# A decoder block in float32 on one core: every stage of cross-attention behind the row scaling runs one slot sooner

## What is computed

```python
x = x + attn(layernorm(x))            # 16 heads of 64, over each batch's 128 tokens
x = x + xattn(layernorm(x), ctx)      # 16 heads of 16, keys and values from ctx, a mask over keys
x = x + ffn(layernorm(x))             # 8 experts, 256 -> 512 -> 256, all summed, gated by one norm_g
```

## Time and profile before

| | |
|---|---|
| median of 3 runs | 855.11 us (855.07 to 857.67) |
| the profiled execution: its time | 854.01 us |
| the profiled execution: its span | 852.2 us |
| busy share of the span | PE 96%, PEld 83%, ACT 56%, DVE 53%, POOL 27% |
| mean granted TensorE clock | 0.992 of full |
| first and last scores of cross-attention (L819) | 320.0 and 466.5 us |

### The profile page before, as it was taken

How to read it: one execution, slowest core, us unless ns; L and a number is a source line. 1 busy time by engine, 2 the same in 40 slices (tenths; PEclk the granted TensorE clock), 3 DMA queues, 4 the chain that set the end, 5 groups by cost and what they waited for, 6 DMA issues and landing times.

```text
span 852.2 us, 16891 instructions
## 1 busy us (share of the span) xinstructions
PE 817.1 (96%) x6171; PEld 711.1 (83%) x6171; DVE 447.7 (53%) x935; ACT 476.8 (56%) x1532; POOL 227.4 (27%) x221
## 2 busy tenths in 40 slices
PE   9999999999999987999887999999999999999998
PEld 7778888888888875777775899999999899999997
DVE  4564664564555548899988554552233322433223
ACT  5555555455464546777777467544544454444543
POOL 3443343123233444668575400000000000000000
PEclk9999999999999999999998999999999999999999
DMA  6311000000000065666471233100000000000000
GB/s 193 108 51 39 1 2 2 2 1 2 2 25 2 2 151 146 167 144 179 99 195 51 62 100 99 50 26 2 1 1 2 25 0 0 0 25 1 1 1 25
DMA packets 22889, 42.22 MB, mean 50 GB/s; under 512 B 3352, under 2 KB 3872, under 8 KB 22816
## 3 DMA queue, kind: packets, MB, share of 16 engines
q1 hardware_dynamic: 21936, 40.64, 17.6%
q10 hardware_dynamic: 880, 0.60, 0.3%
HBM read 30.35 MB, written 10.49 MB: 48 GB/s over the span
## 4 chain that ended last, share of the span: by engine, by line
PE 81%; DVE 9%; DMA 3%; issue 3%; ACT 2%; POOL 2%; SPq 0%; POOLq 0%; ACTq 0%; DVEq 0%
PE Y L720 27%; PE A L720 25%; PE S L720 11%; PE T L847 5%; PE S L838 3%; PE O L881 3%; ACT probs L1127 2%; DMA arena<-stage 2%; DVE probs L1300 1%; DVE nm L1291 1%; PE S L819 1%; DVE xn L1231 1%; DMA stage<-arena 1%; PE O L868 1%; PE S L949 1%
## 5 line engine op out<-in xcount | busy, mean ns | idle before, releaser
L1127 ACT ACTIVATE probs<-S,nm 128x128 f32<-128x128 f32 x512 | 180.5, 378 | 127.3 <-DVE nm L1291 127.2
L720 PEld LDWEIGHTS Y<-arena,PT 128*128 128x128 f32 x1536 | 199.9, 191 | 11.4 <-DVE PT L1203 1.4
L1203 DVE TENSOR_TENSOR PT<-probs,PT 128x512 fp32r<-128x512 f32 x128 | 89.7, 702 | 227.5 <-ACT PT L1183 227.5
L720 PE MATMUL Y<-arena,PT 128*128 128x256 f32 x1536 | 203.8, 283 | 0.4
L1551 POOL TENSOR_TENSOR probs<-probs,rinv 128x512 f32<-128x512 f32 x128 | 134.3, 1049 | 236.3 <-DVE rinv L1296 236.3
L720 PE MATMUL A<-XT,arena 128*128 128x512 f32 x612 | 159.2, 394 | 0.0
L1183 ACT ACTIVATE PT<-probs 128x512 fp32r<-128x512 f32 x128 | 80.8, 631 | 106.9 <-PE Y L720 106.5
L1300 DVE COPY probs<-T 128x512 f32<-128x512 f32 x96 | 66.0, 688 | 113.3 <-PE T L847 112.9
L720 PEld LDWEIGHTS A<-XT,arena 128*128 128x128 f32 x612 | 108.1, 189 | 17.9
L1127 ACT ACTIVATION_READ_ACCUMULATOR probs<-S,nm 128x1 f32 x512 | 111.2, 217 | 0.0
L720 PE MATMUL S<-XT,arena 128*128 128x512 f32 x384 | 99.7, 395 | 0.0
(11 more groups left out here) (124 smaller groups left out, 996.4 us busy)
## 6 DMA issues: line engine op xcount, KB each, us to landing
wst<-in_pieces SPq DMA_DIRECT2D x43, 256.0 KB, 2.6
stage<-arena SPq DMA_DIRECT2D x32, 256.0 KB, 2.8
arena<-stage SPq DMA_DIRECT2D x51, 128.0 KB, 3.9
arena<-stage SPq DMA_DIRECT2D x21, 256.0 KB, 3.9
craw<-in_ctxT SPq DMA_DIRECT2D x4, 512.0 KB, 4.1
out<-craw SPq DMA_DIRECT2D x8, 256.0 KB, 2.0
xs<-in_x SPq DMA_DIRECT2D x3, 512.0 KB, 5.4
craw<-in_pieces SPq DMA_DIRECT2D x6, 256.0 KB, 2.6
```

The lines of the kernel that those rows point to most:

```text
L720: mm = pe.matmul(acc, lhs[a], rhs[b], start=first and i == 0, stop=last and i == 2, skip_group_check=shared)
L1127: last = act.activation(probs[:, ring(ph, g, n), u * P:(u + 1) * P], S[n % 2][:, u * P:(u + 1) * P], ACT.Exp, bias=nm[:, n % 4, u:u + 1], ...
L1203: dve.tensor_tensor(out_, src, hi.bitcast(F32), ALU.subtract).then_inc(sem_, 1)
```

## The change

In the phase 1 stages behind the normalisation, every lag goes down by one: the transposes from 3 to 2, the copies from 4 to 3, PV, `out` and `out_hi` from 5 to 4, `out_low` from 6 to 5, projection, residual and bias from 6 to 5. The scores, maxima, exponentials, inverses and the normalisation keep theirs, and so does the place of each stage in its engine's order within a slot. No instruction is added or removed, and no semaphore is changed. The diff of the tables (where an entry stands for several like it, one is shown):

```diff
         PE_ORDER = (
...
-            (("pv", "cross", (0, 5)), ("scores", "cross", (0, 0)), ("proj", "proj", (3, 6)),
+            (("pv", "cross", (0, 4)), ("scores", "cross", (0, 0)), ("proj", "proj", (3, 5)),
              ("xt1", "xt1", (0, 0)), ("v", "v", (0, 0)), ("qk", "qk", (0, 0)),
-             ("xt0", "xt0", (0, 0)), ("transpose", "cross", (0, 3))),
+             ("xt0", "xt0", (0, 0)), ("transpose", "cross", (0, 2))),
...
         DVE_ORDER = (
...
-            (("probs", "cross", (0, 4)), ("inverse", "cross", (0, 2)), ("out", "cross", (0, 5)),
+            (("probs", "cross", (0, 3)), ("inverse", "cross", (0, 2)), ("out", "cross", (0, 4)),
              ("max", "cross", (0, 0)), ("xt1", "xt1_out", (0, 0)),
              ("qk", "q_out", (0, 0)), ("xt0", "xt0_out", (0, 0)), ("stats", "stats", (0, 0)),
-             ("aggr", "aggr", (0, 0)), ("norm", "norm", (0, 0)), ("residual", "residual", (3, 6))),
+             ("aggr", "aggr", (0, 0)), ("norm", "norm", (0, 0)), ("residual", "residual", (3, 5))),
...
         POOL_ORDER = (
-            (("normalise", "quad", (1, 2)), ("out_hi", "cross", (0, 5)), ("out_low", "cross", (0, 6)),
-             ("bias", "bias", (3, 6)), ("aggr", "aggr", (0, 0)),
+            (("normalise", "quad", (1, 2)), ("out_hi", "cross", (0, 4)), ("out_low", "cross", (0, 5)),
+             ("bias", "bias", (3, 5)), ("aggr", "aggr", (0, 0)),
              ("ctx", "ctx", (0, 0))),
```

More of the change, by code:

```diff
@@ L513, in build @@
              ("scores", "even", (0, 0)), ("pv", "odd", (1, 0)), ("transpose", "even", (1, 0)),
-             ("proj", "proj", (3, 6))),
-            (("pv", "cross", (0, 5)), ("scores", "cross", (0, 0)), ("proj", "proj", (3, 6)),
+             ("proj", "proj", (3, 5))),
+            (("pv", "cross", (0, 4)), ("scores", "cross", (0, 0)), ("proj", "proj", (3, 5)),
              ("xt1", "xt1", (0, 0)), ("v", "v", (0, 0)), ("qk", "qk", (0, 0)),
[1 row of a table removed]
[1 row of a table added]
             (("xt1", "xt1", (0, 0)), ("qk", "qk", (0, 0)), ("v", "v", (0, 0)), ("xt0", "xt0", (0, 0))),
-            (("scores", "cross", (0, 0)), ("proj", "proj", (3, 6)), ("pv", "cross", (0, 5)),
-             ("transpose", "cross", (0, 3)), ("v", "v", (0, 0)), ("qk", "qk", (0, 0))),
-            (("transpose", "odd", (1, 0)), ("proj", "proj", (3, 6)), ("v", "v", (0, 0)),
+            (("scores", "cross", (0, 0)), ("proj", "proj", (3, 5)), ("pv", "cross", (0, 4)),
+             ("transpose", "cross", (0, 2)), ("v", "v", (0, 0)), ("qk", "qk", (0, 0))),
+            (("transpose", "odd", (1, 0)), ("proj", "proj", (3, 5)), ("v", "v", (0, 0)),
              ("pv", "odd", (1, 0)), ("scores", "cross", (0, 0))),
@@ L538, in build @@
              ("qk", "q_out", (0, 0)), ("max", "even", (0, 0)), ("out", "odd", (1, 0)),
-             ("inverse", "even", (0, 0)), ("out_low", "odd", (1, 0)), ("residual", "residual", (3, 6)),
+             ("inverse", "even", (0, 0)), ("out_low", "odd", (1, 0)), ("residual", "residual", (3, 5)),
              ("stats", "stats", (0, 0)), ("aggr", "aggr", (0, 0)), ("norm", "norm", (0, 0))),
-            (("probs", "cross", (0, 4)), ("inverse", "cross", (0, 2)), ("out", "cross", (0, 5)),
+            (("probs", "cross", (0, 3)), ("inverse", "cross", (0, 2)), ("out", "cross", (0, 4)),
              ("max", "cross", (0, 0)), ("xt1", "xt1_out", (0, 0)),
              ("qk", "q_out", (0, 0)), ("xt0", "xt0_out", (0, 0)), ("stats", "stats", (0, 0)),
-             ("aggr", "aggr", (0, 0)), ("norm", "norm", (0, 0)), ("residual", "residual", (3, 6))),
+             ("aggr", "aggr", (0, 0)), ("norm", "norm", (0, 0)), ("residual", "residual", (3, 5))),
             (("xt1", "xt1_out", (0, 0)), ("qk", "q_out", (0, 0)),
@@ L547, in build @@
              ("xt0", "xt0_out", (0, 0))),
-            (("inverse", "cross", (0, 2)), ("out", "cross", (0, 5)), ("probs", "cross", (0, 4)),
+            (("inverse", "cross", (0, 2)), ("out", "cross", (0, 4)), ("probs", "cross", (0, 3)),
              ("max", "cross", (0, 0)), ("qk", "q_out", (0, 0)),
-             ("residual", "residual", (3, 6)), ("stats", "stats", (0, 0)), ("aggr", "aggr", (0, 0)),
+             ("residual", "residual", (3, 5)), ("stats", "stats", (0, 0)), ("aggr", "aggr", (0, 0)),
              ("norm", "norm", (0, 0))),
@@ L555, in build @@
         POOL_ORDER = (
-            (("normalise", "quad", (1, 2)), ("out_hi", "cross", (0, 5)), ("out_low", "cross", (0, 6)),
-             ("bias", "bias", (3, 6)), ("aggr", "aggr", (0, 0)),
+            (("normalise", "quad", (1, 2)), ("out_hi", "cross", (0, 4)), ("out_low", "cross", (0, 5)),
+             ("bias", "bias", (3, 5)), ("aggr", "aggr", (0, 0)),
              ("ctx", "ctx", (0, 0))),
-            (("normalise", "quad", (1, 2)), ("out_hi", "cross", (0, 5)), ("out_low", "cross", (0, 6)),
-             ("bias", "bias", (3, 6)), ("aggr", "aggr", (0, 0)),
+            (("normalise", "quad", (1, 2)), ("out_hi", "cross", (0, 4)), ("out_low", "cross", (0, 5)),
+             ("bias", "bias", (3, 5)), ("aggr", "aggr", (0, 0)),
              ("ctx", "ctx", (0, 0))),
             (("aggr", "aggr", (0, 0)),),
-            (("normalise", "quad", (1, 2)), ("out_hi", "cross", (0, 5)), ("out_low", "cross", (0, 6)),
-             ("bias", "bias", (3, 6)), ("aggr", "aggr", (0, 0)),
+            (("normalise", "quad", (1, 2)), ("out_hi", "cross", (0, 4)), ("out_low", "cross", (0, 5)),
+             ("bias", "bias", (3, 5)), ("aggr", "aggr", (0, 0)),
              ("ctx", "ctx", (0, 0))),
-            (("normalise", "quad", (1, 2)), ("blank", "blank", (0, 0)), ("out_hi", "cross", (0, 5)),
-             ("out_low", "cross", (0, 6)), ("ctx", "ctx", (0, 0))))
+            (("normalise", "quad", (1, 2)), ("blank", "blank", (0, 0)), ("out_hi", "cross", (0, 4)),
+             ("out_low", "cross", (0, 5)), ("ctx", "ctx", (0, 0))))
         block = ctx.enter_context(nc.Block())
```

## The result

The changed kernel takes 893.2 us (median of four runs, 891.6 to 894.9) against 856.3 beside it: 1.042 times the time of the kernel before, interval 1.038 to 1.046. Run again it gave 1.0419 (1.0391 to 1.0447). The forecast was 885.5 with a range of 869 to 901. The profiled execution took 891.6 with a span of 889.8, which is 37.6 over the span of before.

What follows compares the result with a forecast made beforehand. PE was taken as nearly the bound before, a one-slot ring of 2.64 us after the change. Terms of 16.9, 8.5, 0.5, 1.1 and 3.4 sum to 30.4; with 855.1 that gave 885.5 us, range 869 to 901.

Steps and rivals of the forecast that it cites:

- term 1: The 48 steady slots each hold the whole ring of 2.64 us: 126.7 us against 109.84, +16.9.
- a ring of one slot: Normalisation, transposes, copy and inverse wait for each other within one slot, 2.64 us; before, the ring closed over two slots.
- Term 2: Crowded slots 0, 6, 12 (14 in the second group) and 15 outlast the ring and no longer average out: +8.5.
- Term 3: The opening: quad 0's transposes stand before quad 3's scores, one set of 0.56 us in that path: +0.5.
- Term 4: The drain, to the last transposes: they come one slot sooner, but longer slots use that up: +1.1.
- Term 5: Behind the last transposes: only one expert block runs beside the output chain, PE waits before the projection: +3.4.
- The fall of the clock: Rival: PE's waits lower its clock for some three slots in each of four passes, +12, 897 us; chance 0.13.
- "Faster": Rival: the ring's links overlap, under 2.29 us, and the pipeline ends one slot sooner: 853 us; chance 0.02.
- "even": Rival: only light slots feel the ring and the terms cancel against a sooner end, within 2.6 us; chance 0.02.
- The normalisations: Sign: their starts stand 2.6 to 2.7 us apart in plain slots, 3.8 to 4 in slots 6 and 12.

Runs made afterwards that it cites:

- one swap: VectorE's inverse put ahead of the copy in the changed kernel: 867.8 us, 1.016; the same in the kernel before: 853.7 us, 0.997.
- a dose: GpSimd's normalisation in two halves, 1.18 us for 1.04: on the changed kernel 899.9 us, 1.0515; on the kernel before 852.2 us, 0.997.
- the repeat: The changed kernel run once more with nothing altered: 892.4 us, 1.0419.
- the filler: Changed kernel plus unused matmuls of ones before drain transposes: 890.7 us, 1.040; placed again (eight before quad 10, none before 11, 15): 891.1 us, 1.0405.

## Why the prediction was right, and where it was short

- **The mechanism and term 1** held: a ring of one slot, 2.64 us forecast, 2.64 to 2.65 measured, opened by one swap and, in plain slots, lengthened one for one by a dose.
- **Term 2** was forecast at 8.5; over 48 x 2.64 the stretch took 9.5. Most crowded slots came out as costed. In slot 6 the residual now follows the low half:

```profile
395.74 0.74 DVE L1275 SCALAR_TENSOR_TENSOR arena<-A,bias,arena 128x512 fp32r<-128x512 f32 x1
396.40 1.28 DVE L1331 TENSOR_TENSOR xs<-Y,xs 128x512 f32<-128x512 f32 x2
397.60 0.68 DVE L1300 COPY probs<-T 128x512 f32<-128x512 f32 x1
398.19 0.17 DVE L1296 RECIPROCAL rinv<-rsum 128x4 f32<-128x4 f32 x1
```

  From normalisation to normalisation there (394.67 to 398.44) are 3.77, +1.13 as forecast. Slot 12 gave +1.19 and +1.22 for +1.28, but +0.67 in the last group's pass, where no context is left to cast and only the power stands before the normalisation. Slot 15 gave +0.59 for +0.64, and slot 0 had the short pair of xn, GpSimd being idle (in slot 15, with `out_low` on GpSimd, it was 2.22):

```profile
379.04 1.09 DVE L1231 TENSOR_SCALAR xn<-xs,mv,rstd 128x256 f32<-128x256 f32 x2
```

  What I hadn't counted are two small ones, 0.19 in slot 2 (PE's projection and transposed tokens) and 0.17 in slot 14 (GpSimd's `out_hi` and context), and one slot in the fourth group's pass in which the clock fell: 3.91 for 2.64. Taking each pass where its clock held, apart from the opening's tail, 44.5 and 45.6 us here and 44.9 in the repeat, the 48 slots come to 134.9, against 135.2 forecast. That is closer than the parts deserve: the 0.6 too much for the last slot 12 and the 0.7 of small ones left out nearly cancel. In the five profiles of this stretch the clock fell one to three times, 0.9 to 1.3 us each.
- **Term 3** was short, 0.5 for 2.0. I priced a set of transposes only. They stand ahead of the next scores, and they waited for a normalisation that itself stood behind layernorm's power; PE's clock had fallen in that wait (it falls in the opening of the kernel before as well, 0.50 in 332:334):

```profile
330.69 1.11 PE L847 MATMUL T<-ident,probs 128*128 128x128 f32 x4 [2.13 <-POOL probs L1551]
331.74 1.08 PE L868 MATMUL O<-probs,wst 128*32 128x128 f32 x16
...
332.75 0.80 PE L819 MATMUL S<-dropped,identr 128*128 128x512 f32 x1
```

  How much of the 2.0 is the change stays open: in the five profiles of the changed opening the second group's first maximum comes at 331.9 to 334.4, in the one of before at 332.0.
- **Term 4** was the worst, 1.1 for 4.2, and the failed step is the clock, which I had put into a rival as something that comes in every pass or not at all. It fell in the drain. There normalisations stood 3.10 apart where the transposes ran at half speed, and the last transposes came 4.09 us after those before them, since an expert block at the lower clock took 2.78 us (503.68) where 1.64 is usual, ahead of them. With the clock held up that step was 3.0; the 0.4 over the ring is the last normalisation, 1.40 us for 1.04. Another 0.4 is VectorE's expert low half in slot 4, which I took to fit, and the slot that crosses the first cut has 0.6 of xn in it, which this sum left out. So the clock is about 2 of the 3 us that were missing. With the filler the drain still took 35.5, 2.5 over the kernel before.
- **Term 5** was 4.4 for 3.4. With the clock held up 3.05 of it stay (13.85 less 10.80), and with the projection back in its place 0.9. The term was right in kind and in size; a fall of the clock lay on top.
- **The rivals.** The fall of the clock came true in part: four to six of the 37 us by the cuts above, not 12, in the drain, the end, the opening and one slot of the steady part. Only the drain's and the end's share was tried with a run. In the passes a fall cost about 1 us, where the rival had three slots of 1 us each. Most of the steady stretch kept full clock with PE busy for 81% of it, as the stretch from 452 to 460 before had suggested. "Faster" and "even" had no ground: no slot under 2.64 in the ring.
- **The sum**, 30.4, was 7 short of 37. One is in the ring's slots, the other six in the opening, the drain and the end.
- **The signs.** The normalisations did as said. The maxima didn't: they follow each other at 3.20 and 2.09 us in turn, 2.00 at the least, where 2.6 to 2.7 and none under 2.5 was the sign, and 1.4 to 2 was to speak against the theory. This sign contradicts the prediction's own term 2, by which a slot with PV has its maximum 0.57 later: 2.64 + 0.57 and 2.64 - 0.57. PE's wait for the normalisation was to be some 0.5 us in nearly each slot and over 20 in all; it was about 1 us in 25 of the 48, 25.5 in all. Of the 60 copies between the first cut and the last transposes 40 are recorded as waiting for the transposes, not each. PE's wait at the end was 1.42 for some 2.

## What to carry to other kernels

In a software pipeline written slot by slot, before a stage is moved one slot sooner, follow the orders of all engines and look for rings: work of quad n that waits for work of n-1 through in-order queues. Add the latencies once round and divide by the slots that the ring spans; that quotient is a floor under the mean slot, whatever the engines' busy shares say. If the ring spans a single slot it also ends the averaging of heavy and light slots, so count the heavy ones separately. Which of two stages stands first in an engine's slot can decide whether the ring exists: here it was worth 22 to 25 us in the changed kernels and 2 to 3, at the edge of what can be told, in the one with a slot to spare.

## What the runs showed of the hardware beyond that

The links between engines are steady: in plain slots at full clock, in the drain and the passes alike, the normalisations start 2.64 or 2.65 us apart, so this chain's price could be summed from single rows with an error of a hundredth.

In the changed kernel's trace the granted clock fell to its lower level, 1.2 GHz, in or shortly behind a wait of PE of 1.4 to 2.1 us: 2.13 before 330.69, 0.50 in 330:332; 1.94 before the transposes at 445.14 and 0.50 in 446:448; 1.91 before 485.26 and 0.50 in 488:490; 1.98 before 503.26 and 0.50 in 504:506; 1.42 before the projection at 514.38 and 0.50 in 518:520. Such a wait doesn't bring the fall each time, and the same program differs from one execution to the next. Waits of 1.94 and 2.02 before 399.54 and 416.62 left the clock at 1.00 here; in the repeat the same two (1.94 and 2.01) were followed by 0.50 in 401:403 and 418:420. In the ring a slot at the lower clock cost 0.45 us where only the transposes lie in it (3.10 for 2.65) and 1.3 where a block of PE's projections stood ahead of them. The clock came back after PE had been busy without a break: in 446:449, 492:496 and 504:507.
